# Six products with one sparse-valued matrix: from one row of tiles per product to sweeps in which a split tile serves two products

## The reference

```
u = x
for _ in range(3):
    v = mlp(adj @ u, uv_W1, uv_b1, uv_W2, uv_b2, uv_W3, uv_b3)
    u = mlp(adj @ v, vu_W1, vu_b1, vu_W2, vu_b2, vu_W3, vu_b3)   # the last u is not used
x = layernorm(x + v)
x = layernorm(x + adj @ (x @ gcn_W))
```

## Time and profile before

| | us |
|---|---|
| median of 3 runs (lowest, highest) | 1229.32 (1228.2, 1230.36) |
| the profiled execution's own time | 1229.88 |
| its span in the profile | 1227.9 |
| PE busy, share of the span | 1206.0, 98% |
| DVE busy, share | 1005.8, 82% |
| ACT busy, share | 873.1, 71% |
| read from HBM, mean rate | 394.73 MB, 323 GB/s |
| granted TensorE clock, mean | 0.997 |

### The profile page before, as it was taken

One profiled execution on the slowest core, in us unless ns is written; L12 is line 12 of the kernel. 1 busy time (PEld: TensorE's weight loads), 2 busy tenths in 40 slices (PEclk: granted clock), 3 DMA queues, 4 the chain that ended last, 5 costly groups with the idle time before them and its releaser, 6 DMA issues.

```text
span 1227.9 us, 13400 instructions
## 1 busy us (share of the span) xinstructions
PE 1206.0 (98%) x5376; PEld 969.5 (79%) x5376; DVE 1005.8 (82%) x624; ACT 873.1 (71%) x690; POOL 11.0 (1%) x29
## 2 busy tenths in 40 slices
PE   6999999999999999999999999999999999999997
PEld 5788778877887788778877887787778787788886
DVE  4888888888888888888888888888888888787884
ACT  4777777777777777777777777777777777677773
POOL 2000000000000000000000000000000000000000
PEclk9999999999999999999999999999999999999999
DMA  8899998798889798989878899978888886799992
GB/s 344 319 359 346 352 341 341 273 352 341 340 340 351 274 341 340 352 342 340 334 292 339 341 341 351 342 271 324 303 322 311 314 323 238 287 371 345 365 362 88
DMA packets 56365, 397.69 MB, mean 324 GB/s; under 512 B 6544, under 2 KB 6672, under 8 KB 8432
## 3 DMA queue, kind: packets, MB, share of 16 engines
q1 hardware_dynamic: 55440, 394.88, 85.2%
q0 software_dynamic: 864, 1.97, 0.4%
HBM read 394.73 MB, written 2.10 MB: 323 GB/s over the span
## 4 chain that ended last, share of the span: by engine, by line
PE 96%; ACT 1%; DMA 1%; DVE 1%; issue 0%; SPq 0%; ACTq 0%; DVEq 0%
PE acc L530 85%; PE layer L473 6%; PE proj L479 3%; DMA raw<-adj_dram 1%; PE minus_mean L491 1%; PE var L497 1%; ACT high L223 1%; PE spread L511 1%; DVE low L350 1%; ACT squared L257 0%; SPq L151 0%; DVE p_low L383 0%; ACT p_high L266 0%; SPq L157 0%; DVE h L371 0%
## 5 line engine op out<-in xcount | busy, mean ns | idle before, releaser
L350 DVE TENSOR_TENSOR low<-raw,high 128x2048 fp32r<-128x2048 f32 x372 | 846.9, 2292 | 182.6 <-ACT high L223 181.8
L223 ACT ACTIVATE high<-raw 128x2048 fp32r<-128x2048 f32 x372 | 712.2, 1915 | 84.2 <-PE acc L530 75.9
L530 PE MATMUL acc<-high,p_low 128*128 128x512 f32 x1536 | 644.3, 419 | 9.0 <-DVE low L350 6.9
L530 PE MATMUL acc<-low,p_high 128*128 128x512 f32 x1536 | 601.2, 391 | 0.0
L530 PE MATMUL acc<-high,p_high 128*128 128x512 f32 x1536 | 600.8, 391 | 0.0
L530 PEld LDWEIGHTS acc<-high,p_low 128*128 128x128 f32 x1536 | 289.4, 188 | 89.1 <-issue 30.6
L530 PEld LDWEIGHTS acc<-high,p_high 128*128 128x128 f32 x1536 | 289.5, 188 | 79.1 <-issue 22.8
L530 PEld LDWEIGHTS acc<-low,p_high 128*128 128x128 f32 x1536 | 289.0, 188 | 62.0
L238 ACT ACTIVATE z<-layer,b_uv_b 128x512 f32<-128x512 f32 x48 | 33.1, 690 | 70.1 <-PE layer L473 70.1
L355 DVE SCALAR_TENSOR_TENSOR h<-z 128x512 f32<-128x512 f32 x120 | 82.7, 689 | 0.0
L227 ACT ACTIVATE p_high<-proj 128x512 fp32r<-128x512 f32 x40 | 23.9, 599 | 69.0 <-PE proj L479 69.0
(11 more groups left out here) (45 smaller groups left out, 259.2 us busy)
## 6 DMA issues: line engine op xcount, KB each, us to landing
raw<-adj_dram SPq DMA_DIRECT2D x372, 1024.0 KB, 5.2
resid<-x_t_dram SPq DMA_DIRECT2D x8, 256.0 KB, 15.7
kept<-adj_dram SPq DMA_DIRECT2D x2, 1024.0 KB, 16.3
out_t_dram<-z POOLq DMA_DIRECT2D x3, 256.0 KB, 5.3
out_t_dram<-normed POOLq DMA_DIRECT2D x3, 256.0 KB, 5.4
out_t_dram<-z SPq DMA_DIRECT2D x1, 256.0 KB, 2.1
out_t_dram<-normed SPq DMA_DIRECT2D x1, 256.0 KB, 2.0
w_vu_W<-vu_W_dram POOLq DMA_DIRECT2D x3, 64.0 KB, 6.8
```

The lines of the kernel that those rows point to most:

```text
L223: nc.scalar.activation(high[slot][:], source[:], ACT.Copy).then_inc(high_ready, 1)
L350: nc.vector.tensor_tensor(low[slot][:], source[:], high[slot][:].bitcast(F32), ALU.subtract).then_inc(low_ready, 1)
L530: done = nc.tensor.matmul(acc[side][:], part[parity][:, at:at + D], adj_part[slot][:, columns], start=(g == 0 and j == 0 and i == 0), stop ...
```

## The change

The numbers of a product and its matmuls stay (6 x 8 chunks x 96). What changes:

- **Tiles** have 2 blocks (128 x 1024, 512 KiB), 16 for a row of `adj`. `raw` has 5 buffers, `high` and `low` 8 each. A *visit* is one tile for one product: 6 matmuls. There are 6 x 8 x 16 = 768 visits, numbered n.
- **Sweeps.** A tile once split can be visited by two products k and k+1, where P of product k+1 is already there. The first sweep does product 0 whole and the part of product 1 below the diagonal; sweep k (1 to 4) finishes product k and begins k+1; the last finishes product 5. A partial sum is moved out of PSUM to `part` in SBUF (ACT `keep`, or DVE `grow`, which adds to it) and later added to the rest (DVE `finish`, into `total`). PSUM has 4 accumulating banks.
- **The order** is made by `Plan`: a list of visits, and for each chunk a visit `start`, right behind the last visit of its sum (`SPACING` sets chunks apart). The steps of its tail stand at fixed visits after `start`. Each engine goes through the same n = 0, 1, 2, ... and emits at each n its chunk steps first, then `keep` or `grow`, then the splits of the tiles that PE opens at n + 6 (`AHEAD`).
- **Bias and leaky** are one ACT operation, `Prelu`, done twice for layers 1 and 2 (once rounded to fp32r, once not); DVE subtracts the two. The **dense layers** 2 and 3 are then three fp32r passes. The projections stay plain fp32.
- **Layernorm**: PE transposes the chunk (4 transposes), DVE takes mean and variance with `bn_stats` and `bn_aggr`, ACT takes the root, and ACT applies scale and shift. The centering is folded into the weight of the last projection.

The core of the diff:

```diff
+PER_TILE = 2
+RAWS = 5
+SLOTS = 8
+AHEAD = 6
+BANKS = 4
+HELD = 6
+LOWER_1, LAYER_2, LOWER_2, LAYER_3, PROJECT, P_LOWER = 1, 3, 4, 6, 8, 9
+ADD_X, TURN, ROOT, SCALE, NORMALIZE, NORM_P_LOWER = 7, 9, 10, 11, 12, 12
+SPACING = [2] * NORMED + [4, 3]
+LAST_TURN, LAST_MEASURE, LAST_ROOT, LAST_SCALE = 2, 2, 3, 4
...
+    def both(self, chunk, columns, first, second, held):
+        kept = []
+        for i, column in enumerate(columns):
+            t = self.tile(chunk, column)
+            self.visit(t, first)
+            if i < len(columns) - held:
+                self.visit(t, second)
+            else:
+                kept.append(t)
+        for t in kept:
+            self.visit(t, second)
...
+    def first_sweep(self):
+        for c in range(CHUNKS):
+            whole = self.open(0, c, "whole")
+            self.one(c, self.band(range(c, CHUNKS)), whole)
+            if c:
+                self.both(c, self.band(range(c)), whole, self.open(1, c, "keep"), HELD if c == CHUNKS - 1 else 0)
+    def sweep(self, k):
+        rows = list(range(CHUNKS)) if k % 2 == 0 else list(range(CHUNKS))[::-1]
+        def corner(r, goal):
+            self.one(rows[r], self.band([rows[r]]), self.open(k, rows[r], goal))
+        for r in (1, 2, 3):
+            corner(r, "more")
+        corner(0, "finish")
+        self.one(rows[1], self.band(rows[:1]), self.open(k, rows[1], "finish"))
+        for r in (4, 5, 6):
+            corner(r, "more")
+        made = self.one(rows[2], self.band(rows[:2]), self.open(k, rows[2], "finish"))
+        self.one(rows[1], self.band(rows[:1]), self.open(k + 1, rows[1], "keep"))
+        second = self.open(k + 1, rows[2], "keep")
+        for t in made:
+            self.visit(t, second)
+        for r in range(3, CHUNKS - 1):
+            first = self.open(k, rows[r], "finish")
+            self.both(rows[r], self.band(rows[:r]), first, self.open(k + 1, rows[r], "keep"), 0)
+        first = self.open(k, rows[-1], "whole")
+        self.one(rows[-1], self.band(rows[-1:]), first)
+        self.both(rows[-1], self.band(rows[:-1]), first, self.open(k + 1, rows[-1], "keep"), HELD)
...
+            def load(t):                                    # SP
+                if t >= RAWS:
+                    sp.wait_ge(low_ready, t - RAWS + 1)
+                sp.dma_start(raw[t % RAWS][:], adj[tiles[t][0], tiles[t][1]]).then_inc(raw_loaded[t % RAWS], 16)
...
+            def rectify(source, bias, i):                   # ACT
+                nc.scalar.activation(h_high[i % 2][:], source, ACT.Prelu, bias=bias, alpha=SLOPE)
+                return nc.scalar.activation(h[i % 2][:], source, ACT.Prelu, bias=bias, alpha=SLOPE)
+            def first_layer(i):
+                if finishes(i):
+                    act.wait_ge(total_ready, sums[chunks[i].total].nth + 1)
...
+                for i, chunk in enumerate(chunks):          # ACT, at each n
+                    if layered(i):
+                        if n == chunk.start:
+                            first_layer(i)
...
+                for s in sums:
+                    if s.goal == "keep" and n == s.read:
+                        keep(s)
+                for t in range(len(tiles)):
+                    if n == split_at[t]:
+                        split(t)
...
+            def split(t):                                   # DVE
+                dve.wait_ge(high_ready, t + 1)
+                nc.vector.tensor_tensor(low[t % SLOTS][:], raw[t % RAWS][:], high[t % SLOTS][:].bitcast(F32),
+                                        ALU.subtract).then_inc(low_ready, 1)
+            def finish(i):
+                nc.vector.tensor_tensor(total[:], acc[chunks[i].total % BANKS][:], part[:, blocks_of(s.chunk)],
+                                        ALU.add).then_inc(total_ready, 1)
+            def lower_first(i):
+                dve.wait_ge(first_ready, i + 1)
+                nc.vector.tensor_tensor(h_low[i % 2][:], h[i % 2][:], h_high[i % 2][:].bitcast(F32),
+                                        ALU.subtract).then_inc(first_lowered, 1)
+            def measure(i, source):
+                for j in range(IN_CHUNK):
+                    nc.vector.bn_stats(stats[:, j, :], block_in(source, j)).then_inc(stats_ready, 1)
+                for j in range(IN_CHUNK):
+                    dve.wait_ge(stats_ready, (i - NORM) * IN_CHUNK + j + 1)
+                    done = nc.vector.bn_aggr(moments[:, j, :], stats[:, j, :])
+                done.then_inc(moments_ready, 1)
...
+            def dense(name, i):                             # PE
+                nc.tensor.matmul(layer[i % 2][:], w_low[name][:], h_high[i % 2][:], start=True, stop=False)
+                nc.tensor.matmul(layer[i % 2][:], w_high[name][:], h_high[i % 2][:], start=False, stop=False)
+                return nc.tensor.matmul(layer[i % 2][:], w_high[name][:], h_low[i % 2][:], start=False, stop=True)
```

More of the change, by code:

```diff
@@ L1 @@
 from contextlib import ExitStack
+from dataclasses import dataclass
 import concourse.bass as bass
@@ L40, in gnn_kernel @@
 def gnn_kernel(nc, adj, x_t, weights, biases, out_t):
+    plan = Plan()
+    tiles, visits, sums, chunks = plan.tiles, plan.visits, plan.sums, plan.chunks
+    END = len(visits) + 16
     with ExitStack() as ctx:
@@ L132, in kept_of, with way_of @@
[L132 to L141, removed]
+        def way_of(i):
+            return "uv" if sums[chunks[i].total].product % 2 == 0 else "vu"
@@ new lines, in finishes, with layered, plain, normed @@
+        def finishes(i):
+            return sums[chunks[i].total].goal == "finish"
+        def layered(i):
+            return i < FINAL
+        def plain(i):
+            return i < NORM
+        def normed(i):
+            return NORM <= i < FINAL
+        def split_before(t):
+            return max(0, plan.opening[t] - AHEAD, plan.closing[t - SLOTS] + 1 if t >= SLOTS else 0)
+        split_at = [split_before(t) for t in range(len(tiles))]
+        def made_by(product, chunk):
+            if product == 0:
+                return chunk + 1
+            return CHUNKS + 1 + next(i for i, c in enumerate(chunks) if sums[c.total].product == product - 1
+                                     and sums[c.total].chunk == chunk)
@@ L143, in gnn_kernel, with over_with @@
+        def over_with(product, chunk):
+            return 1 + max(n for n, v in enumerate(visits) if sums[v.total].product == product
+                           and v.column // IN_BAND == chunk)
         block = ctx.enter_context(nc.Block())
@@ new lines, in _ @@
+            load_x(0)
+            load(0)
+            load_x(1)
+            for t in range(1, RAWS):
+                load(t)
+                if t % IN_BAND == 0:
+                    load_x(t // IN_BAND + 1)
+            for t in range(RAWS, len(tiles)):
+                if t % IN_BAND == 0 and t // IN_BAND + 1 < CHUNKS:
+                    load_x(t // IN_BAND + 1)
+                load(t)
+            for i in (len(chunks) - 2, len(chunks) - 1):
+                sp.wait_ge(normed_ready, i - NORM + 1)
+                sp.dma_start(out_t[sums[chunks[i].total].chunk], h[i % 2][:]).then_inc(last_stored[i % 2], 16)
@@ new lines, in multiply @@
+            def multiply(n):
+                v = visits[n]
+                s, slot = sums[v.total], v.tile % SLOTS
+                if n == plan.opening[v.tile]:
+                    pe.wait_ge(low_ready, v.tile + 1)
+                if n == s.opens and v.total >= BANKS:
+                    wait_bank(v.total)
+                pe.wait_ge(p_low_ready, made_by(s.product, v.column // IN_BAND))
+                parity, bank = s.product % 2, acc[v.total % BANKS]
+                for j in range(PER_TILE):
+                    at = (v.column * PER_TILE + j) * D
+                    columns = slice(j * CHUNK, (j + 1) * CHUNK)
+                    for m, (p, a) in enumerate(((p_low, high), (p_high, high), (p_high, low))):
+                        done = nc.tensor.matmul(bank[:], p[parity][:, at:at + D], a[slot][:, columns],
+                                                start=(n == s.opens and j == 0 and m == 0),
+                                                stop=(n == s.closes and j == PER_TILE - 1 and m == 2))
+                done.then_inc(visited, 1)
```

828 lines of the change are left out of this document (412 added, 416 removed).

## The result

The changed kernel takes 1257.61 us (median; 1256.03 to 1258.93), the kernel before 1228.76 in the same rounds: ratio 1.0233, 95% interval 1.0215 to 1.0251, 29 us slower. The forecast was 1231 with a range of 1200 to 1248. It was missed by 27 us.

A forecast was written before the change was run, and what follows sets the result against it. The prediction took PE to bound the kernel: from the profiled 1229.88 us, savings of 52.4 and +0.25 for the centred weight gave 1177.7, and new waits of 53.4 made 1231 us; range 1200 to 1248.

The forecast's parts named there:

- The bound and the PE account: Whole kernel: PE, busy 98%, is the bound; work and waits leaving its path come to -52.4 us.
- Dense layers: Layers 2 and 3 of 40 chunks: three fp32r passes take 0.68 us for 0.90, -17.6 us in all.
- The layernorm: Products 4 and 5: four transposes at 0.44 us replace about 2.3 us a chunk; 15 chunks save 28.2 us.
- The shapes: Operation times read off other sizes: half tile 1.22 us on DVE, 1.04 on ACT; bn_stats 0.28, double Prelu 1.28.
- The junctions: Four passages between sweeps: PE waits for late lowerings, 2.9 and 2.5 us the longest; 7.15 each, 28.6 together.
- The last sweep: From visit 690: DVE's 120 us of work plus late start and idling make 128 where PE needs 112.4: +15.5 us.
- The ring: Five half-tile raw buffers: a load must land within 4.1 us; 3.8 was taken, so no wait.
- rival C: Ring of five half tiles: loads landing in 5.2 us cost the first sweep 17 us; 1248 us, chance 0.21.
- The start: Kernel start through chunk 0: 40.7 us after the change against 43.96 before, -3.3 us.
- the forecast's own: Whole kernel: the forecast's range without the rivals, 1221 to 1242 us, chance 0.36.
- Rival B: Junctions and last sweep: PE stays the bound, waits in all under 25 us; 1195 us, chance 0.33.

The follow-up runs named there:

- E8: The kernel before with Prelu on ACT and dense layers in three fp32r passes, no sweeps or new layernorm: 1210.04 us, ratio 0.9853.
- E4: The changed kernel with one plain fp32 matmul for each dense layer in place of three fp32r passes: 1272.23 us, ratio 1.0357.
- E9: The kernel before with Prelu, three-pass dense layers and the layernorm by transposes and bn_stats, no sweeps: 1190.91 us, ratio 0.9684.
- E2: The changed kernel with 12 unused filler matmuls put on PE ahead of each of 11 long waits: 1258.79 us, ratio 1.0248.
- E1: The changed kernel with DVE's two lowerings of a chunk moved ahead of the split of their visit: 1235.16 us, ratio 1.0053.
- E5: The changed kernel with ACT's normalize of a final chunk issued behind the split of its visit: 1250.42 us, ratio 1.0184.
- E3: The changed kernel with adj tile loads, but for the first five, cut to 128 of 1024 columns: 1248.62 us, ratio 1.0164.
- E6: The changed kernel with seven raw buffers in place of five and seven high and low slots in place of eight: 1255.3 us, ratio 1.0218.
- E7: The changed kernel with lowerings ahead of the split, normalize behind it, seven raw buffers and seven slots: 1220.9 us, ratio 0.9939.

## Why the prediction was wrong

**The bound and the PE account: right.** Nothing but PE was on the path before. Dense layers: 17.6 forecast, 18 measured alone (E8), 14.6 inside the change (E4). The layernorm: 0.44 per chunk forecast, 0.49 measured in product 4 (E9). E9 over E8 gives 19 us of the 28 even so: some 6 of the rest went in the last product, by the waits to loads, and almost 5 in products 0 to 3, where a chunk took 24.18 us for E8's 24.03, which isn't explained. The shapes: 1.22 and 1.04 us for the half tiles, 1221 and 1054 ns measured; bn_stats 0.28, measured 0.285; the double Prelu 1.28, measured 1.34 from `total` and 1.27 from PSUM. Root and Prelu don't alternate table loads: two in the kernel, as before.

**The junctions: the mechanism right, the sum nearly.** 2.9, 2.5, 1.0 and 0.25 were forecast. Measured 2.95, 0.66 (2.24 at full clock, E2), 1.11 and 0.24. E1 shows the mechanism: the same work in another order takes 5.1 us off each sweep. Some luck is in the 2.9: the terms that are added up to 24.2 give 24.5, and the wait would be 3.2. And the fallen clock behind the long wait, 2.7 us a sweep, was no term; it made up for what the second wait was short of. Each sweep still came 1.7 us over.

**The last sweep: the step that failed.** "72 splits (85) ... 120, plus 2.5 late start and some 1.5 of idling." DVE's work was 110 us in 144, so less than the 120; the idling was not 1.5 but some 34. The sum has DVE's invert and shift as 0.35 us of work and nothing behind them. But ACT's list has `normalize` at that same visit ahead of its split, waiting for this very shift: 2.67 us of DVE idling at each of the seven final chunks, 19 us. It is the pattern that the walk did count at the junctions (Prelu ahead of split), left out where another name stood in the list. PE's waits for `total` and for normalize in this stretch came to 21 us, with matmuls at the lower clock behind them, where 15.5 were forecast for the whole. Of the 15.9 us over, E5 takes back 5.8 and the loads 4.9 to 5.0 (E3, E6); E7, with E1's order on top, takes back 12.7. The last 3.2 are open.

**The ring: rival C's mechanism, half its size and in another place.** The forecast took 3.8 us to landing and no wait, with 4.1 as the point from which it decides; loads landed in 4.5, over its lower estimate of 3.2 too. Light loads gave back 9.0 us, not C's 17, and at the start and the end, not across the first sweep: visits 16 to 178 took 241.1 us with either loads, 1.3 over the forecast, although the loads of visits 16 to 100 landed in 4.7 us. The half tile's landing was derived from the right rows, and the value taken (3.8) lay on the comfortable side of the threshold for no reason in them: the row of 5.8 for 1 MiB less 1.2 gave 4.6.

**The start.** -3.3 was forecast, from 40.7 after and 43.96 before. The 43.96 was misread: the matmul that starts there opens the last tile of chunk 0, and the second chunk begins twelve matmuls later:

```profile
46.55 0.39 PE L530 MATMUL acc<-low,p_high 128*128 128x512 f32 x1
46.78 0.39 PE L530 MATMUL acc<-high,p_low 128*128 128x512 f32 x1
```

So by its own working the term should have been -6.1; measured it is +0.4 (visit 16 at 47.1 against 46.8). Three things make up most of the 6.4 us between 40.7 and 47.1. The first matmul came at 12.8 (11.8 to 12.8 in the runs), not 11.7, and that is again the order of ACT's list: before, the first split stands between the copies of the first two x chunks, after the change behind both. The second x chunk itself came no later (PE begins on it at 7.87, before at 8.16). ACT before, then after:

```profile
7.32 1.91 ACT L223 ACTIVATE high<-raw 128x2048 fp32r<-128x2048 f32 x1 [0.26 <-DMA raw<-adj_dram]
10.27 0.60 ACT L227 ACTIVATE p_high<-proj 128x512 fp32r<-128x512 f32 x1 [1.04 <-PE proj L479]
...
9.98 0.60 ACT L384 ACTIVATE p_high<-flip 128x512 fp32r<-128x512 f32 x1 [2.50 <-PE flip L648]
10.47 2.94 ACT L380 ACTIVATE high<-raw 128x1024 fp32r<-128x1024 f32 x3
```

The prediction named both copies and still took over the 11.7 of a list with one. Next, the first 12 matmuls all went at 0.43 us (5.3 us, 4.2 before). Last, the loads account for about 3: PE waits 2.15 us at visit 4 for the P of the third x chunk, whose copy stands on ACT behind splits that wait for loads; with light loads that wait is gone.

**Rival B** (the covers hold) falls: PE's waits on `h_low` and `total` came to some 42 us, over the 25 that it allowed. **The chances**: 0.43 for slower, but the range stopped at 1248 with the forecast's own at 1242. It let the forecast and C each move the time alone. Both came true in part, at once.

## What to carry to other kernels

Where two engines split one tile between them, everything that one list holds ahead of its half stalls the other: before a move, write both lists for each n side by side, and put a step that the third engine waits for ahead of the split, a step that is not needed soon behind it. Taking a quarter of its work from DVE, which was never the bound, bought nothing: E9, without the sweeps, is 30 us faster than E7 with them (they also differ in tile size and buffers). What the sweeps cost is, as I read it, the regularity that hid DVE and ACT. When several waits are priced from one walk, an omission in it hits all alike, so the range must hold a doubled wait total, not only the rivals one by one.

## What the runs showed of the hardware

- From visit 178 on, PE had nine waits of 2.95 to 4.96 us. Behind eight of them the granted clock fell to 1.2 GHz for 6 to 12 matmuls (0.43 us apart), then rose to 2.4 again; behind one of 3.19 it didn't, nor behind any of 1.6 or less. A wait of 2.24 (E2) was followed by it once, waits of 2.29 and 2.26 were not. Filling the waits with matmuls kept it up at most places (E2, 0.995 for 0.982), yet saves time only if nothing else is late behind it.
- Three fp32r passes of 512 columns take 0.68 us on PE's path (E8); one plain fp32 matmul in their place 0.90 (the kernel before; in E4 they cost 14.6 us more in 80 layers).
- `bn_stats` on 128x128 took 285 ns from PSUM and 281 from SBUF, `bn_aggr` 153 ns; a Prelu of 128x512 rounding to fp32r 688 ns from PSUM, 724 from SBUF.
- A half tile of 512 KiB landed in 4.5 us with five buffers in the ring and with seven (E6), 64 KiB in 1.8 (E3).
